# Second attention of a four-layer fused kernel: the steps of the next layer's routing, and one batch's eight scatters, in other places of the order

## The reference

```
x = x + tanh(g_xattn[1]) * attention1(layernorm(x), ctx, ctx, mask)      # 16 heads of 8, 32 keys, softmax
x = x + tanh(g_ffn[1]) * moe1(layernorm(x))

moe1: probs = softmax(x @ router_w.T)            # 8 experts
      top 2 of them, their probs divided by their sum
      y = sum over the two: prob * (gelu(x @ w_fc[e] + b_fc[e]) @ w_proj[e] + b_proj[e])
```

## The kernel before

| step | engine and function | what it does |
|---|---|---|
| mom | DVE `moments3` L1875, POOL `rsqrt3` L703 | mean and variance; power and a small product (L706, L708) |
| scl | ACT `norm3` L921, `copy_rows` L930 | normalised rows (L927), and a second copy (L934) |
| xt | PE `rows_in1` L1481, ACT `rows_t1` L937 | four transposes into T (L1485), copy out (L939) |
| logits | PE `logits1` L1488 | four small products into T |
| shift, exp | DVE `shift_route1` L1972, ACT `exp_route1` L941 | softmax's maximum and exponential (L943) |
| top, mark | DVE `choose_route1` L1982, `mark_route1` L1991 | probabilities, the two largest, their weights |
| cum | PE `cumulate1` L1494 | running count of rows per expert into T |
| slots | DVE `slots` L2175 | row numbers and gates (L2184 to L2199) |

## Time and profile before

### The profile page before, as it was taken

One profiled execution on the slowest core, in us unless ns is written; L12 is line 12 of the kernel. 1 busy time (PEld: TensorE's weight loads), 2 busy tenths in 40 slices (PEclk: granted clock), 3 DMA queues, 4 the chain that ended last, 5 costly groups with the idle time before them and its releaser, 6 DMA issues.

```text
span 888.9 us, 14103 instructions
## 1 busy us (share of the span) xinstructions
PE 757.4 (85%) x3936; PEld 538.1 (61%) x3936; DVE 558.4 (63%) x1813; ACT 373.4 (42%) x832; POOL 390.4 (44%) x381
## 2 busy tenths in 40 slices
PE   6999879999989876785899687999989887988885
PEld 3477756666767554554889686565655453655553
DVE  3378677878788375755433575978778644524554
ACT  0244234444444434532446334546456555213331
POOL 2000034545456443354564343655356663245661
PEclk8799979999999978976799899999999999899998
DMA  5022999800000311003776751000320000022325
GB/s 142 1 72 86 340 331 333 262 1 1 0 1 1 84 29 25 18 25 98 226 208 188 203 166 35 26 1 1 107 74 10 13 13 13 17 55 79 90 52 142
DMA packets 74396, 79.36 MB, mean 89 GB/s; under 512 B 17769, under 2 KB 61424, under 8 KB 74194
## 3 DMA queue, kind: packets, MB, share of 16 engines
q1 hardware_dynamic: 68112, 69.49, 27.0%
q0 software_dynamic: 5024, 8.54, 2.9%
q10 hardware_dynamic: 1186, 0.43, 0.2%
HBM read 40.48 MB, written 39.85 MB: 90 GB/s over the span
## 4 chain that ended last, share of the span: by engine, by line
PE 54%; DVE 21%; issue 10%; POOL 6%; ACT 4%; DMA 3%; SPq 1%; ACTq 0%; POOLq 0%; DVEq 0%
PE psum L1169 49%; POOL y L745 3%; DVE hb L2304 2%; DVE hb L2305 1%; POOL s L740 1%; DVE hb L2302 1%; DVE mr L1969 1%; PE psum L1688 1%; PE psum L1228 1%; DMA chosen<-in_mask_1x1xSxS_ik 1%; PE psum L1356 1%; DVE x L1942 1%; DVE const L1925 1%; DMA l_hi<-y 1%; DMA s<-l_hi,l_lo 1%
## 5 line engine op out<-in xcount | busy, mean ns | idle before, releaser
L677 POOL TENSOR_TENSOR h_lo<-hb,h_hi 128x512 fp32r<-128x512 f32 x68 | 87.8, 1293 | 121.4 <-ACT h_hi L905 121.3
L1169 PE MATMUL psum<-xt_hi,wa_hi 128*128 128x512 f32 x272 | 127.7, 470 | 13.0 <-DVE hb L2305 8.2
L745 POOL DMA_INDIRECT y<-xn x93 | 92.1, 990 | 82.8 <-DVE xn L2061 41.7
L887 ACT ACTIVATE hb<-psum 128x512 f32<-128x512 f32 x136 | 81.0, 596 | 81.7 <-PE psum L1169 81.6
L1169 PE MATMUL psum<-xt_lo,wa_hi 128*128 128x512 f32 x272 | 107.6, 396 | 0.0
L672 POOL TENSOR_TENSOR hb<-hb,wsb 128x512 f32<-128x512 f32 x64 | 82.6, 1291 | 53.3 <-DVE hb L2302 46.2
L1169 PEld LDWEIGHTS psum<-xt_hi,wa_hi 128*128 128x128 f32 x272 | 52.2, 192 | 35.7 <-DVE hb L2305 13.9
L1169 PE MATMUL psum<-hb,wa_hi 128*128 128x512 f32 x136 | 70.0, 595 | 0.5 <-POOLq L674 0.5
L2302 DVE TENSOR_TENSOR hb<-hb,psum 128x512 f32<-128x512 f32 x68 | 46.0, 685 | 37.7 <-ACT hb L887 27.8
L1169 PE MATMUL psum<-l_lo,l_hi 128*128 (+1 forms) x204 | 57.1, 380 | 10.8 <-issue 5.7
L648 POOL TENSOR_TENSOR rstd<-veps,neghalf 128x4 f32<-128x4 f32 x20 | 20.3, 1016 | 97.1 <-DVE veps L1863 96.3
(11 more groups left out here) (352 smaller groups left out, 1708.1 us busy)
## 6 DMA issues: line engine op xcount, KB each, us to landing
s<-l_lo SPq DMA_DIRECT2D x20, 1386.0 KB, 16.7
l_hi<-in_pack SPq DMA_DIRECT2D x24, 322.0 KB, 3.4
l_lo<-in_pack SPq DMA_DIRECT2D x22, 322.0 KB, 3.5
xn<-s SPq DMA_DIRECT2D x93, 66.0 KB
stage<-in_pack SPq DMA_DIRECT2D x13, 256.0 KB, 2.6
y_in<-y SPq DMA_DIRECT2D x8, 256.0 KB, 3.8
l_hi<-y SPq DMA_DIRECT2D x8, 256.0 KB, 4.8
stage<-in_L_ffn_W SPq DMA_DIRECT2D x12, 128.0 KB, 2.4
```

Source lines behind the costliest of these rows:

```text
L677: pool.tensor_tensor(h_lo[:, k % 3, :], hb[:, k % 4, :], h_hi[:, k % 3, :].bitcast(F32), ALU.subtract).then_inc(q["hlo_pool"], 1)
L745: pool.indirect_dma_start(y3, bass.IndirectOffsetOnAxis(xe3[:, j % XE, 128:129].bitcast(I32), 0), xe3[:, j % XE, 0:128], None, bounds_chec ...
L887: act.activation(hb[:, k % 4, :], G[k % 2][:, :], ACT.Silu).then_inc(q["sg_done"], 1)
L1169: return pe.matmul(o, l, r, start=start, stop=stop, skip_group_check=True)
```

## The change

The tables of steps get other numbers, and some calls get another place within a tile:

- Batch 0: normalised rows at tile 6 instead of 5, transposes at 8 (6), logits at 9 (7), shift, exp and choosing at 10 (7, 7, 8), marks at 11 (8), the running count and the slots at 12 (8 and 10). Its scatters are issued at 12, 13 and 14 instead of 11 to 14.
- Batch 1: scl 10 (9), xt 11 (10), logits 12 (11), shift and exp 13 (11), choosing and marks 13 (12), count and slots 14 (12 and 13). All eight scatters are issued at step 15; before, one at 14, three at 15 and four at 16.
- Batches 2 and 3: moments of batch 2 at 15 (14); from there every step is one to two numbers later, and the logits of batch 2 move from step 16 to 18, so into the expert loop.
- The three parts of the block tables are made at steps 15, 16, 17 on PE (13, 15, 16) and 15, 16, 17 on DVE (14, 15, 16) for the first half, and one or two steps later for the second.
- `logits1` is always issued at the end of a tile. `shift_route1` of batches 0 and 1 is issued before `shift1(i + 3)`, `exp_route1` of batches 0 and 1 at the head of a tile, and `cumulate1(0)` before the transposes of tile 12.
- `update` is issued before `shift1(i + 3)`, `query1` before `values1`, and in DVE's `chain1` the block tables before the moments.

```diff
--- before.py
+++ after.py
@@ -58,11 +58,11 @@
 XL = 5
 SKIP = 1 << 20
 LOOP1 = 18
-STEP1 = dict(mom=(5, 9, 14, 16), scl=(5, 9, 14, 17), xt=(6, 10, 15, 18), logits=(7, 11, 16, 19), shift=(7, 11, 16, 19),
-             exp=(7, 11, 16, 19), top=(8, 12, 17, 20), mark=(8, 12, 17, 21), cum=(8, 12, 18, 22), slots=(10, 13, 18, 23))
-SCAT1 = [(11, 11, 12, 12, 13, 13, 14, 14), (14, 15, 15, 15, 16, 16, 16, 16), (19, 19, 20, 20, 21, 21, 22, 22), tuple(range(24, 32))]
-COUNT1 = [(13, 15, 16), (24, 26, 28)]
-TABLE1 = [(14, 15, 16), (25, 27, 29)]
+STEP1 = dict(mom=(5, 9, 15, 16), scl=(6, 10, 16, 18), xt=(8, 11, 17, 19), logits=(9, 12, 18, 20), shift=(10, 13, 18, 20),
+             exp=(10, 13, 18, 20), top=(10, 13, 19, 21), mark=(11, 13, 19, 22), cum=(12, 14, 20, 23), slots=(12, 14, 20, 24))
+SCAT1 = [(12, 12, 13, 13, 13, 14, 14, 14), (15,) * 8, (21, 21, 22, 22, 23, 23, 24, 24), tuple(range(25, 33))]
+COUNT1 = [(15, 16, 17), (25, 27, 29)]
+TABLE1 = [(15, 16, 17), (26, 28, 30)]
 TAP1 = 17
 SPEC1 = [LOOP1 + 12 + 2 * i for i in range(5)]
 FFT1 = dict(add0=32, mom0=33, add1=34, rows0=35, to0=36, mom1=36, mul0=37, back0=38, rows1=38, upd0=39, mom5=40, to1=40, mul1=41,
@@ -950,7 +950,7 @@
                         copy_rows(n)
                     if g == STEP1["xt"][n]:
                         rows_t1(n)
-                    if g == STEP1["exp"][n]:
+                    if g == STEP1["exp"][n] and g > 15:
                         exp_route1(n)
                 if g == TAP1 + 1:
                     act.wait_ge(q["w_ps"], 1)
@@ -1106,6 +1106,9 @@
                         exp1(i)
                     for i in range(16):
                         b, k = divmod(i, TB)
+                        for n in range(HALF):
+                            if i == STEP1["exp"][n]:
+                                exp_route1(n)
                         if i + 3 < 16:
                             exp1(i + 3)
                         prob_t1(i)
@@ -1506,9 +1509,9 @@
                 for n in reversed(range(B)):
                     if g == STEP1["xt"][n]:
                         rows_in1(n)
-                    if g == STEP1["logits"][n] and g > 15:
+                    if g == STEP1["logits"][n]:
                         logits1(n)
-                    if g == STEP1["cum"][n]:
+                    if g == STEP1["cum"][n] and n:
                         cumulate1(n)
                 if g in COUNT1[0] and g <= 15:
                     block_counts(COUNT1[0].index(g), 0, sel1, E1)
@@ -1760,19 +1763,17 @@
                     scores1(2)
                     for i in range(16):
                         b, k = divmod(i, TB)
-                        for n in range(B):
-                            if i == STEP1["logits"][n]:
-                                logits1(n)
                         if i + 3 < 16:
                             scores1(i + 3)
+                        if i == STEP1["cum"][0]:
+                            cumulate1(0)
                         probs_t1(i)
+                        if b + 1 < B and k == 0:
+                            query1(b + 1)
                         if i >= 1:
                             values1(i - 1)
-                        if b + 1 < B:
-                            if k == 0:
-                                query1(b + 1)
-                            if k == 2:
-                                value1(b + 1)
+                        if b + 1 < B and k == 2:
+                            value1(b + 1)
                         if b + 2 < B and k == 3:
                             xt_in(2, b + 2)
                         chain1(i)
@@ -2001,14 +2002,14 @@
 
             def chain1(g):
 
-                for n in reversed(range(B)):
-                    if g == STEP1["mom"][n]:
-                        moments3(n)
                 for part in range(2):
                     if g in TABLE1[part]:
                         block_table(TABLE1[part].index(g), part, E1)
                 for n in reversed(range(B)):
-                    if g == STEP1["shift"][n]:
+                    if g == STEP1["mom"][n]:
+                        moments3(n)
+                for n in reversed(range(B)):
+                    if g == STEP1["shift"][n] and g > 15:
                         shift_route1(n)
                     if g == STEP1["top"][n]:
                         choose_route1(n)
@@ -2490,11 +2491,14 @@
                         b, k = divmod(i, TB)
                         if i + 1 < 16:
                             sums1(i + 1)
-                        if i + 3 < 16:
-                            shift1(i + 3)
                         if k == 1 and b >= 1:
                             dve.wait_ge(q["pv_ps"], 4 * b)
                             update(s, b - 1, ACC, tg[:, 1:2])
+                        for n in range(HALF):
+                            if i == STEP1["shift"][n]:
+                                shift_route1(n)
+                        if i + 3 < 16:
+                            shift1(i + 3)
                         if k == 1 and b + 2 < B:
                             moments(s, b + 2)
                         if k == 2 and b + 2 < B:
```

## The result

The changed kernel took 880.0 us in the median (878.41 to 881.90, four runs) beside 894.69 for the kernel before (four runs): a ratio of 0.9841, with a 95% interval of 0.9803 to 0.988. Timed again beside the last experiments, it took 883.11 (877.59 to 887.60, twelve runs) against 893.03 (seventeen runs): 0.9907, interval 0.9872 to 0.9942. So the gain is 14.7 us by the first comparison and 9.9 by the second, larger one; the forecast was 10.5 and 884.5 us.

A forecast was written before the change was run, and what follows sets the result against it. In the second attention no engine is full, so order was taken to set the time. Gain 12.6 - 2.0 - 0.1 for ACT = 10.5 us, off a median of 895.05: 884.5 us, range 878 to 893.5.

The forecast's parts named there:

- scores and slots: Second attention: scores of tile 10 at 346.3 and of tile 15 at 366.9; batch 0's slots done at 372.6.
- the landing: Batch 1's last scatter arrives, before the expert loop reads rows: 399.5 instead of 412.1, 12.6 us earlier.
- the hand-offs of T: Expert loop start: routing steps of batches 2 and 3 waiting for PE's bank T are covered; cost 0, uncovered 2.3 us.
- the tail: Attention's last tiles, POOL and DVE late: attention ends at 387 to 390 against 402.8; first of eight scatters 387.1 to 389.3.
- The case that PE falls to 1.2 GHz: End of attention: PE's work after tile 15's multiply ends at 388.0 with the slower clock, 385.8 at 2.4 GHz.
- the 2.0 us that the loop was to give back: Expert loop: later POOL scatters delay write-backs whose slots row loads reuse; 2.0 us charged, bounds 0 and 4.
- The 0.1 for ACT: Deduction in the sum for ACT, whose two possible added table loads had bounds 0 and 2.6 us, taken as 0.
- full gain: Rival: attention's end stays at full clock and the loop hides all; 13.7 us gained, 881.3 us, chance 0.16.
- Attention not shorter: Rival: another chain takes over; the scatters in one piece alone gain 5.0, less 2.0 in the loop; 892.0 us, chance 0.15.
- Table loads: Rival: two added ACT table loads show before a gelu PE waits for; 2.6 us on the sum, 887.1 us, chance 0.08.
- POOL holds the loop: Rival: scatters of batches 2 and 3 delay the second half's rows in the expert loop; 905.5 us, chance 0.09.
- the early update of the first step (337.25): Second attention, near PE's tile 4: with the update ahead of `shift1` it is done at 337.25.

The follow-up runs named there:

- the last experiments: Changed kernel with batch 1's eight scatters ahead of batch 2's moments: 875.36 us; with throwaway products in PE's waits as well: 876.02 and 876.24 us.
- filler: Kernel with the scatters ahead of batch 2's moments, plus useless PE products in the tile 6 wait: 876.02 us; also ahead of tile 12's values: 876.24 us.
- the split piece: Changed kernel with batch 1's eight scatters cut into four at step 15 and four at step 16: 882.64 us, ratio 0.9883.
- the exponential first: Changed kernel with batch 3's exponential on ACT ahead of the first gelu, single run: 882.66 us.

## Why the forecast held, step by step

**Right: scores and slots.** Tile 10's scores were forecast at 346.3 and stand at 344.81, 346.3 with the head's 1.5 put back. Tile 15's: 366.9 forecast, 366.7 in the same count. Batch 0's slots end at 371.2, 372.7 in that count, forecast 372.6. The tile sum (scores, transposes, values, extras) carried. No wait of DVE in this stretch is over 2.47 us (384.90), where 6.86 stood. Behind the landing the hand-offs of T cost nothing, as forecast: the first gelu is 12.2 us earlier than before, the fourth 13.9.

**Mis-sized: the tail.** The range for the first of the eight scatters was 387.1 to 389.3, and the middle was taken; in the same count it stands at 390.3. (The terms as written land at 398.2 to 400.4; the printed 398.4 to 400.6 is 0.2 more.) The case that PE falls to 1.2 GHz, given as the upper end, is what happened, and on top of it POOL's multiply of tile 15 came 0.8 us later than 380.3 and 0.52 us passed between the small product and the first issue. The landing was forecast at 399.5 and is 400.1, 401.6 with the head put back: a gain of 12.0 as the traces stand, but 10.5 net, where 12.6 was the term.

**Failed: the 2.0 us that the loop was to give back.** The steps up to it were right: batch 2's scatters begin 14.5 us behind the landing, POOL's free time shrank, and the waits of SyncE's row loads for write-backs grew from 9.2 us in eight to this (total, number, longest):

```profile
SPq L522 <- DMA y<-xn: 13.1, 9, 4.1
```

Only the last inference fell: these loads were early enough. Gelu of block 18 is 12.4 us earlier than before and the output 11.5, against 12.0 at the landing; and moving the write-backs up did nothing. By the end 0.7 us net were lost, where 2.0 had been charged. One pair of traces cannot tell 0.7 from nothing: from the start of the last scatter to the end it is 479.1 us before and 479.8 in the changed kernel, but 478.5 to 482.0 over the fourteen traces. Their means, 480.2 in the three with the order of before in the loop and 479.9 in the eleven with the new, show no 2.0. The 0.1 for ACT in the sum has no working, and its paragraph takes 0; no run shows it.

**What was luck.** 2.1 us too much at the landing and 1.3 too much taken off behind it have opposite signs, and this is why the sum, 10.5, came out near the 9.8 of the traces and the 9.9 of the second comparison. The first comparison's 14.7 is nearest to the full gain's 13.7, a rival whose full clock in the tail the trace refutes.

**The rivals.** *Full gain*: its loop was nearly right (0.7 lost), its full clock in the tail wrong. *Attention not shorter*: refuted by the times of tiles 10 to 15; its price for the piece, 5.0, was a miscount of the six issues, two of which were batch 0's; the trace shows 2.3 (the runs, 1.4 to 7.3, decide nothing here). *Table loads*: the two more appeared, as the Trainium skill's "ScalarE activation tables: per-element evaluation and per-set limits" (What a function is on this engine) has it, each 1.28 us; leaving them out gained nothing in the one trace that does. *POOL holds the loop*: batch 3's last scatter begins at 445.42, which with 2.3 us is 47.6 behind the landing (forecast 48), block 23's rows are loaded 54.0 behind it.

**Not in the forecast: the update's hoist.** It stands in the prediction only as the early update of the first step (337.25), without a price of its own. Without it the change loses 6.7 us at the landing of its one trace, where the wait that returns takes the clock with it; by the runs 3 to 9.

## What to carry to other kernels

Where a wait of some 2 us stands in PE's order, price it with the slower work that can follow it and not by its own length alone: here, in one trace, 1.88 us of waiting cost over 6, while an equal wait earlier in it cost no clock. Before a burst of DMA issues, look for what the issuing engine waits for just ahead of them and whether the burst needs it; one normalisation moved behind the burst was worth 4 us at the landing. And compare traces from a place ahead of the change: two executions of one kernel stood 4.8 us apart before the changed code began.

## What was not expected

The same wait, in the same place, sometimes costs the clock and sometimes does not. The changed kernel was profiled a second time; its PE at tile 6, to be held against 341.92 and 342.92 above:

```profile
346.77 1.11 PE L1359 MATMUL psum<-const,wk 128*128 128x128 f32 x4 [2.00 <-POOL wk L700]
...
348.53 2.08 PE L1172 MATMUL psum<-xn,wk 128*128 128x128 f32 x8
```

Both wait 2.0 us for POOL. In the first trace the transposes then take 0.66 and the values 1.16, in the second 1.11 and 2.08. The start was 4.8 us late by the head, at the landing it was 7.9: the fall costs 3.1 us. Of the eight traces with this 2.0-us wait ahead of tile 6's transposes and no filler in it, three fell (this one, the split piece and the exponential first) and five did not. Which executions fall, and why, no run here tells. The Trainium skill, in "TensorE: Matmul & The Clock Gate" (Part 1: The HAM clock gate), says that the gate's period runs on by itself and does not start with the kernel; that would let chance decide, and no run here shows it.

The time of a run goes with the mean granted clock: in the second comparison 877.59 us of the changed kernel had 0.936 and 887.60 had 0.927, and of the kernel before 885.15 us had 0.944 and 896.42 had 0.926. The spread of some 10 us of these two kernels goes with the clock, and with it two comparisons of one change can give 14.7 and 9.9 us. The span of the profiled execution of before is 6.2 us under the prediction's median, while after the change a run's time is 879.37 - 877.6 = 1.8 us above its span: the execution profiled before lay some 4 us under its median (an estimate from these two differences). So the spans differ by less than the first medians.
